# Cross attention in a fused two-layer kernel: the projection of the coming queries issued behind the weighted values, the exponential ahead of the query copies, and the scores taken chunk by chunk

## The reference, cut to what matters

```python
q = proj(hs, Wq, bq);  k = proj(at, Wk, bk);  v = proj(at, Wv, bv)    # 16 heads of 16
scores = clip(einsum("bhsd,bhtd->bhst", q, k) / sqrt(16), -50, 50)
scores = where(attention_mask > 0.5, scores, -50)
probs  = softmax(scores);  probs = probs / (probs.sum(-1) + 1e-8)
ctx    = einsum("bhst,bhtd->bhsd", probs, v)
delta  = clip(residual_scale, 0, 0.3) * (ctx @ Wo.T + bo)
x      = x + layernorm(delta) * ln_gamma + ln_beta
```

## Time and profile before

| | value |
|---|---|
| median of three runs | 404.97 us |
| the profiled execution: its own time | 404.29 us |
| its span (first to last instruction) | 402.5 us |
| PE busy | 375.3 us, 93% |
| DVE busy | 287.9 us, 72% |
| ACT busy | 243.8 us, 61% |
| POOL busy | 222.8 us, 55% |
| granted TensorE clock, mean | 0.992 |
| the cross-attention slots 0 to 15 | about 254 to 331 us of the span |

### The profile page before, as it was taken

One profiled execution on the slowest core, in us unless ns is written; L12 is line 12 of the kernel. 1 busy time (PEld: TensorE's weight loads), 2 busy tenths in 40 slices (PEclk: granted clock), 3 DMA queues, 4 the chain that ended last, 5 costly groups with the idle time before them and its releaser, 6 DMA issues.

```text
span 402.5 us, 10051 instructions
## 1 busy us (share of the span) xinstructions
PE 375.3 (93%) x3270; PEld 333.7 (83%) x3270; DVE 287.9 (72%) x836; ACT 243.8 (61%) x563; POOL 222.8 (55%) x376
## 2 busy tenths in 40 slices
PE   6888999899899999999998999899998989999996
PEld 6667888688687888988898999677766879999996
DVE  4869888778878879754445399877878897684633
ACT  4756776276454352467676687866767778653550
POOL 3556555278767674613341568688887766641100
PEclk9999999799999999999999999999999999999999
DMA  7562212122312145547884441121210000010011
GB/s 242 193 184 65 75 43 74 40 65 75 106 66 92 68 166 191 161 140 237 252 268 148 160 130 55 55 65 58 56 48 17 2 2 2 2 53 28 29 52 54
DMA packets 31460, 38.40 MB, mean 95 GB/s; under 512 B 4401, under 2 KB 28594, under 8 KB 31410
## 3 DMA queue, kind: packets, MB, share of 16 engines
q1 hardware_dynamic: 28338, 29.37, 24.0%
q0 software_dynamic: 3072, 8.39, 6.2%
HBM read 25.03 MB, written 12.71 MB: 94 GB/s over the span
## 4 chain that ended last, share of the span: by engine, by line
PE 52%; DVE 15%; POOL 14%; issue 9%; ACT 4%; DMA 4%; SPq 1%; ACTq 0%; POOLq 0%; DVEq 0%
PE PS L331 8%; PE PS L2224 8%; PE PS L2242 8%; PE PS L333 7%; PE PS L332 7%; POOL rows_early L739 4%; DMA raw<-in_w_l 3%; POOL rj L755 2%; POOL raw L739 2%; PE PS L1962 2%; POOL x L764 2%; PE PS L2282 2%; POOL sj L759 1%; PE PS L2300 1%; PE PS L2059 1%
## 5 line engine op out<-in xcount | busy, mean ns | idle before, releaser
L1078 ACT ACTIVATE arena_f<-PS,cols 128x256 f16<-128x256 f32 x64 | 26.5, 472 | 21.6 <-PE PS L2224 19.1
L331 PE MATMUL PS<-wfh,arena_r 128*128 x120 | 36.0, 300 | 3.3 <-DVE arena_f L1578 1.1
L331 PE MATMUL PS<-w0h,arena_r 128*128 128x256 f32 (+1 forms) x96 | 35.1, 365 | 2.1 <-ACT arena_f L901 1.2
L332 PE MATMUL PS<-wfl,arena_r 128*128 x120 | 33.9, 282 | 0.0
L333 PE MATMUL PS<-wfh,arena_r 128*128 x120 | 33.6, 280 | 0.0
L332 PE MATMUL PS<-w0l,arena_r 128*128 128x256 f32 (+1 forms) x96 | 31.3, 326 | 0.0
L333 PE MATMUL PS<-w0h,arena_r 128*128 128x256 f32 (+1 forms) x96 | 31.3, 326 | 0.0
L2224 PE MATMUL PS<-arena_r,w1h 128*128 128x256 f32 x128 | 31.2, 284 | 0.0
L2224 PE MATMUL PS<-arena_r,w1l 128*128 128x256 f32 x128 | 31.0, 283 | 0.0
L475 POOL TENSOR_TENSOR w1l<-raw,w1h 128x384 fp32r<-128x384 f32 (+1 forms) x14 | 12.7, 912 | 32.5 <-ACT w1h L461 32.5
L696 POOL DMA_INDIRECT xs_rows<-rows_early,posi x24 | 24.7, 1031 | 8.9 <-issue 6.7
(11 more groups left out here) (316 smaller groups left out, 1385.0 us busy)
## 6 DMA issues: line engine op xcount, KB each, us to landing
arena_f<-xs_rows SPq DMA_DIRECT2D x40, 128.0 KB, 2.5
ys_rows<-raw SPq DMA_DIRECT2D x20, 256.0 KB, 2.4
raw<-in_w_ffn SPq DMA_DIRECT2D x16, 241.0 KB, 2.7
raw<-in_w_l SPq DMA_DIRECT2D x12, 192.0 KB, 2.9
ctx_raw<-in_ctxT SPq DMA_DIRECT2D x16, 128.0 KB, 2.0
out<-arena_f SPq DMA_DIRECT2D x7, 256.0 KB, 2.1
raw<-in_w_l SPq DMA_DIRECT2D x5, 256.0 KB, 4.6
x<-in_x SPq DMA_DIRECT2D x1, 1280.0 KB, 6.4
```

Source lines behind the costliest of these rows:

```text
L331: nc.tensor.matmul(out_ap, lh, rh, start=first, stop=False)
L332: nc.tensor.matmul(out_ap, lh, rl, start=False, stop=False)
L1078: nc.scalar.activation(md16[:, g % 2, n, :], PS[:, M_H[n // 2], (n % 2) * D:(n % 2 + 1) * D], ACT.Gelu, bias=cols[:, 2 * KC + n:2 * KC + n ...
```

## The change

Three edits, all in the cross-attention slots. On ACT, in odd slots, the Exp of tile s is issued ahead of the four query copies. On PE, in odd slots, the weighted values of tile s-1 are issued ahead of the query projection of the coming pair. In `scores`, the loop over chunks c goes outside the loop over sequences b, and each chunk waits for its own copies: chunk 0 for two of the pair's four, chunk 1 for all four.

```diff
@@ ACT, slot2 @@
                 if (tile := s.tile(-4)) and s.at not in (TILES, TILES + 1):
                     delta(tile[0])
+                if tile := s.tile(0):
+                    probabilities(tile[0])
                 if s.ring == 1 and s.tile(1):
                     queries((s.at + 1) // 2)
-                if tile := s.tile(0):
-                    probabilities(tile[0])
@@ PE, scores @@
-                pe.wait_ge(S2["q_ready"], 4 * (t // 2 + 1))
                 if t >= 2:
                     pe.wait_ge(S2["clipped"], 2 * (t - 1))
-                for b in range(2):
-                    for c in range(KC):
+                for c in range(KC):
+                    pe.wait_ge(S2["q_ready"], 4 * (t // 2) + 2 * c + 2)
+                    for b in range(2):
                         for i in range(2):
@@ PE, slot2 @@
+                if tile := s.tile(-1):
+                    weighted_values(tile[0])
                 if s.ring == 1 and s.tile(1):
                     pair_queries((s.at + 1) // 2)
-                if tile := s.tile(-1):
-                    weighted_values(tile[0])
```

## The result

| | before | changed |
|---|---|---|
| median of 16 runs each | 405.80 us (403.15 to 407.89) | 408.08 us (405.34 to 411.01) |
| profiled execution, its span | 404.29, 402.5 us | 405.84, 404.0 us |
| mean granted clock | 0.992 | 0.992 |

The account below looks back on a forecast made before the run. POOL's instruction order was taken to bound most of the cross-attention stretch. Terms -0.35 + 0 + 0.19 = -0.16 us gave 404.13 by the profiled execution, 404.8 us as median, range 403.4 to 406.2.

Parts of the forecast that it names:

- What bounds the kernel: Cross-attention slots: POOL's own instruction order sets the pace from 258.34 to 305.40 us, then PE 17 us, DVE 8 us.
- rival A: PE as true bound: its 2.4 us of waits for query copies become time saved, 402.6 us as median; chance 7%.
- Term one: Stage entry: scores by chunk let DVE's first clip, and so the whole POOL chain, start earlier: -0.35 us.
- Term two: POOL stretch: later query copies from moving weighted values and Exp stay hidden behind POOL's queue: 0.
- Chunk 1 starts 0.86+0.95+1.98 = 3.79 after the release: Later odd slots: chunk 1's start after POOL releases ACT's norm, against 3.39 needed; even scores 0.40 later against POOL.
- Of which 0.10 is left: Slot 6, tightest place found: moments 0.50 us ahead of POOL's need, 0.10 of that slack remaining, so POOL stays the bound.
- Rival B: Odd slots on ACT: copies come too late, even scores 0.95 later against POOL; +2.7 us, 407.7 as median; chance 5%.
- Rival C: DVE and POOL collide more often, POOL's short gathers turning long: +2.3 us, 407.1 as median; chance 3% slower, 1% faster.
- half: Shared DVE and POOL port: gather rows show half of the 5 us worst case that strict blocking would give.
- Term three: PE stretch at the tail: PE stands before chunk 1 of tile 14's scores, tile 12 without a wait: +0.19 us (0 to 0.4).
- The added waits: One more wait in each of the 16 scores: taken as 0, upper bound 0.35 us.

Follow-up runs that it names:

- r4: Kernel before with the Exp ahead of the query copies and scores by chunk, weighted values not moved: ratio 0.9998 to before, stage 79.46 us.
- e8_wv_chunk: Kernel before with weighted values ahead of the projection and scores by chunk, Exp not moved: ratio 1.0116 to before.
- e11_wait: r4 with the projection in odd slots also waiting for the normalising, weighted values not moved: ratio 1.0015 to the kernel before.
- e3_chunk: Kernel before with only the scores by chunk: ratio 1.0014 to before, stage 81.05 us.
- r1: Kernel before, unchanged, run again on a chip of the experiments: ratio 1.0016, stage 81.05 us.
- e12: r4 with half of the projection computed an extra time ahead of it in odd slots: ratio 1.0109 to the kernel before.
- e10: r4 with DVE's softmax sums and normalising moved ahead of the moments in slot 15 alone: ratio 1.0000 to the kernel before.
- e2_wv: Kernel before with only the weighted values moved ahead of the projection on PE: ratio 1.0142 to before.

## Why the prediction was wrong

**What bounds the kernel** was right: POOL paced the stage up to slot 10, and PE's waits for copies were not time (rival A refuted: they fell by 0.9 us, and the kernel got slower).

**Term one** was right in kind and nearly in size: the clip starts with no idle time before it (254.10, POOL's factor at 257.18), and the entry is 6.11 in place of 6.37: -0.26, I said -0.35.

**Term two** is the step that failed, forecast 0, measured +2.35 us. Two sentences of it were false.
- "Chunk 1 starts 0.86+0.95+1.98 = 3.79 after the release" lets the copies begin right behind the Exp, as if the projection were always done by then. The moved weighted values wait for the normalising of the tile before (1.49, 0.65 and 1.61 us in slots 3, 5 and 7), and their 1.06 us of work follows, both ahead of the projection. That wait is in the listing of the kernel, but my sum read waits off the trace of before, where the projection hid it. From the norm's start to the copies I had 0.86+0.95 = 1.81 us; it is 2.53, 2.14 and 2.13 in slots 3, 5 and 7, and 1.81 in slot 9, where PE waits only 0.24. So the clip of slot 4 is 2.07 behind POOL's factor (before 0.37, without the move 0.98), that of slot 6 1.53 (0.71, 1.20).
- "Of which 0.10 is left" took DVE's way from clip to moments as fixed. It depends on the phase. The Exp's shift was 0.49 in r4, against my 0.40 and a slack of 0.50, so alone it would have been about free; yet r4 waits 1.01 in slot 7, because L1719 took 1.38 us there in place of 0.39. So the wait of slot 7 needs no move at all; what the move adds is the wait of slot 3, most of that of slot 5 (1.06, in r4 0.20) and 0.3 us on POOL's way through slot 6. Of the change's 2.24 us of new waits the longer way from clip to moments gives 0.18 (of 0.43, no more than the wait counted), 0.22 and 0.79: 1.2 us; the rest, 1.05, is lateness proper. That split is by arithmetic; only slot 7's part was tested.

**Rival B** (5%) named the place and the three slots: even scores too late, moments late, POOL waiting in slots 3, 5 and 7. That its +2.7 us is close to the measured 2.8 is luck: it had 1.8 in the POOL stretch and 1.3 behind it, and the stage shows 2.35 and 0.36. It also had the wrong trigger, a late clip that holds the Exp or a chunk split that gives less; the trigger is what stands ahead of the projection, the wait and the moved work. **Rival C** asked the right question on the wrong side. I counted POOL's gathers that grow from 0.94 to 1.16; those of 1.14 us and more between 257 and 304 us went from seven to four. But a gather can be short because it was first, and then it is DVE's operation that waits: by 0.1 to 0.5 us each in the changed kernel, by 0.99 in r4, on the way to the moments.

The collision rule of the Trainium skill (SBUF — State Buffer, section on the two separate sides), by which whoever starts first has the shared ports for its whole instruction and the other blocks fully, I had set aside because a gather grew by only 0.22 beside a 0.47 us operation. For DVE the rows agree with it. The longest hold is in slot 8 of e8_wv_chunk:
```profile
307.32 2.08 DVE L1719 TENSOR_TENSOR arena_f<-arena_f,rows 128x256 f32<-128x256 f32 x1
...
306.70 0.96 POOL L739 DMA_INDIRECT rows_early<-ys_rows,posy  x1 [0.30 <-issue]
307.69 0.73 POOL L764 TENSOR_TENSOR x<-x,rows 128x256 f32<-128x256 f32 x1
308.37 0.73 POOL L769 TENSOR_TENSOR x<-x,arena_f 128x256 f32<-128x256 f32 x1
```
L1719 sits through the gather's end and two whole additions to 309.10, and is done 0.30 later, 0.39 being its full time with the usual overlap of 0.1. In e11_wait it is held through one addition in the same way, 1.23 us, done 0.29 behind it. For the gather as the one that waits, my "half" was a misreading: the gather of the earlier trace rows began 0.14 after the operation, so at most 0.33 us of the 0.47 were left to wait for, and it grew by 0.22.

**Term three** said +0.19 for the tail; it is +0.36, and -0.25 without the move. The scores of tiles 12 and 14 take 1.39 and 1.53 us in place of 1.16; I had tile 12 without a wait. The last weighted values wait for the same normalising, 1.52 us as before. **The added waits** cost nothing that shows: e3_chunk is 1.0014 [0.9975, 1.0052] with the stage of r1; an interval of 0.4% could hide the 0.35 us of my upper bound.

Still open: how the loss splits between the wait and the work (in the POOL part e11 and e12 give roughly half each, by one profiled execution each and blurred by the clock dip; the ratios, 1.0015 and 1.0109, do not split it, since e12's work also costs in the tail); why the waits of slots 5 and 7 come and go from chip to chip in the kernel without the move; and whether a second PSUM place for the weighted values would remove the wait, which was not tried since all eight banks are in use.

## What to carry to other kernels

Before moving an instruction ahead of another, list its waits from the code, not from the trace: a wait that the trace doesn't show may be hidden by just the block that it is moved past. When two engines share a resource in a fixed rhythm, slack is not a number but a phase: ask what an operation will run beside if it comes half a microsecond later, for the one that starts second on either engine. A wait at the end of a stage is worth removing only if nothing else ends at the same time: e10's next layer was waiting for ACT as well. An order that works, as DVE's here, serves two customers, and moving one up moves the other down.

## What the runs showed of the hardware

- An operation on DVE with two SBUF operands (L1719) beside POOL's gather and additions took up to 2.08 us in place of 0.39 (e8_wv_chunk; 1.97 in e2_wv, 1.38 in r4_exp_chunk).
- Whether it is held depends on when it starts. Beside the second gather of a slot, where that takes 0.94 to 0.98 us, 21 such operations in this stage of the 20 profiles began up to 0.30 us into the gather, and none took more than 0.02 us above its usual time; 21 began 0.33 us in or later, and each took longer, by 0.04 to 1.69 us. In slots 4 to 9 of the kernel before, L1636 begins 0.14 or 0.15 ahead of the second gather. Then it is the gather that grows, to 1.14 to 1.17 us, and L1719 behind L1636 is not held.
- The mean granted clock of an execution goes with its time: over 23 executions of before on one of the slower chips from 410.3 us at 0.992 to 417.7 at 0.975, about 3 us per 0.01. There the change also ran at a lower clock (0.975 against 0.984), and its ratio is larger, 1.0098. On the first kind of chip the change's 16 executions average 0.987, and so do the 27 of before on the chip of r4, and the two profiled executions above both have 0.992 with 1.00 in the stage, so the loss there isn't clock.
- Chips differ by 2% for the same kernel, 405.6 us on one and 412.8 to 413.7 on four others, more than the edit cost, so only ratios on one chip were compared. 1.74 us of it lies in this stage (79.31 against 81.05), where r1_before's POOL waits 0.62, 0.66 and 0.42 us for moments in slots 2, 4 and 6, and before's does not.
